# Two attention layers over a shared context: operand q placed by transfers, context normalised on GpSimd, a context load and the ternary weights moved

## The reference, cut to what matters

```
x: 8 x 56 x 128, ctx: 8 x 1500 x 128, 16 heads of 8
x = x + mha(ln(x), ln(x))                    # self-attention over 56 tokens
x = x + mha(ln(x), ln(ctx))                  # first pass: the context is normalised
x = x + mixture of 8 experts(ln(x))          # top 2
# second pass; the context goes in as it is, weights are ternary:
#   Wt = W + (clip(round(W / (mean|W| + eps)), -1, 1) * mean|W| - W)
x = x + mha(ln(x), ctx; weights Wt)
```

## Time and profile before

| | |
|---|---|
| time, median of 3 runs | 639.55 us (637.69 to 640.61) |
| the profiled execution | 638.79 us, of which its span is 637.0 us |
| busy, share of the span | PE 85%, DVE 67%, ACT 51%, POOL 24% |
| chain that ended last | PE 45%, DVE 23%, issue 21%, DMA 4%, POOL 3% |
| granted PE clock, mean | 0.935 |

### The profile page before, as it was taken

One profiled execution on the slowest core, in us unless ns is written; L12 is line 12 of the kernel. 1 busy time (PEld: TensorE's weight loads), 2 busy tenths in 40 slices (PEclk: granted clock), 3 DMA queues, 4 the chain that ended last, 5 costly groups with the idle time before them and its releaser, 6 DMA issues.

```text
span 637.0 us, 16158 instructions
## 1 busy us (share of the span) xinstructions
PE 544.5 (85%) x6582; PEld 383.9 (60%) x6582; DVE 425.6 (67%) x1090; ACT 326.7 (51%) x495; POOL 152.7 (24%) x128
## 2 busy tenths in 40 slices
PE   0699838589999999999967989468999999999996
PEld 0587515266766667676745767234666767667674
DVE  5667478679998999977224302569787687786730
ACT  0165214356666576765743333215566567676573
POOL 1554212313241524300015100223041240421000
PEclk9899668889999999999997989878999999999998
DMA  5010733434436353342200642026536436353300
GB/s 154 32 50 1 164 92 69 126 88 110 132 74 172 72 139 75 75 99 50 100 1 1 170 108 66 9 84 146 137 80 175 121 77 168 88 137 75 74 3 15
DMA packets 25338, 57.44 MB, mean 90 GB/s; under 512 B 4660, under 2 KB 8876, under 8 KB 25268
## 3 DMA queue, kind: packets, MB, share of 16 engines
q1 hardware_dynamic: 25268, 56.45, 34.6%
HBM read 17.81 MB, written 0.23 MB: 28 GB/s over the span
## 4 chain that ended last, share of the span: by engine, by line
PE 45%; DVE 23%; issue 21%; DMA 4%; POOL 3%; ACT 2%; SPq 2%; DVEq 0%; POOLq 0%; ACTq 0%
DVE mxp L791 11%; PE SM L1170 10%; PE PO L1185 9%; PE ST L1149 6%; PE MI L1101 6%; DMA cx<-in_ctx 3%; PE MI L1091 3%; DVE cx L779 3%; DVE qst L815 2%; PE MI L1125 2%; PE SM L1257 2%; DVE ksplit L786 1%; DVE cstat L763 1%; PE SM L1125 1%; DVE xn L732 1%
## 5 line engine op out<-in xcount | busy, mean ns | idle before, releaser
L791 DVE TENSOR_REDUCE mxp<-SM 112x1 f32<-112x500 f32 x364 | 235.2, 673 | 60.5 <-PE SM L1170 59.1
L593 ACT ACTIVATE PT<-ST 128x896 f32<-128x896 f32 x192 | 171.1, 911 | 49.7 <-PE ST L1149 49.1
L1170 PE MATMUL SM<-kst,qst 96*112 96x500 bf16 x364 | 143.1, 407 | 24.7 <-DVE mxp L791 24.1
L1149 PEld LDWEIGHTS ST<-qst,kst 98*128 98x128 bf16 x1536 | 95.0, 100 | 32.6 <-issue 9.7
L1149 PE MATMUL ST<-qst,kst 98*128 98x112 bf16 x1536 | 108.5, 215 | 1.2 <-DMA qst<-mrow 1.2
L471 POOL TENSOR_TENSOR kr<-kf,ksplit 128x500 f32<-128x500 f32 x48 | 56.1, 1170 | 184.4 <-ACT ksplit L565 184.3
L1185 PE MATMUL PO<-PT,vaug 125*32 125x112 f32 x3072 | 96.5, 264 | 2.1 <-ACT PT L593 1.5
L1170 PEld LDWEIGHTS SM<-kst,qst 96*112 96x112 bf16 x364 | 46.8, 131 | 66.9 <-DVE mxp L791 55.2
L1185 PEld LDWEIGHTS PO<-PT,vaug 125*32 125x32 f32 x3072 | 70.5, 110 | 24.5 <-issue 14.9
L577 ACT ACTIVATE vaug<-MI 125x512 f32<-125x512 f32 x48 | 28.7, 598 | 79.4 <-PE MI L1101 79.4
L476 POOL TENSOR_TENSOR ksplit<-kr,ksplit 128x500 bf16<-128x500 f32 x48 | 54.5, 1135 | 53.4 <-DVE ksplit L786 53.4
(11 more groups left out here) (129 smaller groups left out, 555.4 us busy)
## 6 DMA issues: line engine op xcount, KB each, us to landing
kst<-ksplit SPq DMA_DIRECT2D x192, 187.5 KB, 3.8
cx<-in_ctx SPq DMA_DIRECT2D x8, 750.0 KB
xT<-in_ctxT SPq DMA_DIRECT2D x8, 750.0 KB, 4.6
moe<-in_w1T SPq DMA_DIRECT2D x8, 256.0 KB, 2.9
moe<-in_w2T SPq DMA_DIRECT2D x8, 256.0 KB, 3.3
qall<-qsplit SPq DMA_DIRECT2D x12, 112.0 KB, 2.3
watt<-in_watt SPq DMA_DIRECT2D x1, 768.0 KB, 5.8
qst<-mrow SPq DMA_DIRECT2D x32, 1.8 KB
```

Source lines behind the costliest of these rows:

```text
L593: nc.scalar.activation(PT[:, k % PTB], ST[:, k % 2, :, 0:4 * PC], ACT.Exp, scale=SCALE).then_inc(exp_done, 1)
L791: nc.vector.tensor_reduce(mxp[:, j // 3, j % 3:j % 3 + 1], tile_bank(j, banks), AX.X, ALU.max).then_inc(sm_red, 1)
L1149: last = mm(ST[:, k % 2, cc, PC * p:PC * (p + 1)], kst[n.par][:, 4 * half + p, at:at + 128], qst[n.par][:, 4 * half + p], start=True, stop ...
L1170: mm(tile_bank(j, banks), qst[n.par][0:SROWS, j // 3], kst[n.par][0:SROWS, j // 3, at:at + THIRD], start=True, stop=True).then_inc(sm_full, 1)
```

## The change

1. **q by transfers.** For every unit but the first of a pass, SP copies `qall` into `qst` (`place`, two transfers for each half: 48 rows x 4 pairs x 56 bf16). POOL clears `qst` once at the start, so that the zeros are there. PE waits on `q_placed` in place of `qst_ready`.
2. **Normalising on POOL.** The twelve instructions for each of the units 3 to 7 move to POOL, behind `ctx_rstd`. DVE waits for them before it overwrites the statistics in the next window. Units 0 to 2, before the windows, stay on DVE.
3. **Context loads.** In the program a window now loads the context of n + 4, at its end, and unit 3 is loaded before the experts' weights, ahead of the first pass.
4. **Ternary weights** are made in W5, after the tiles of step 6.

```diff
+            def place(n, half):
+                if n.c == 1:
+                    sp.wait_ge(qall_loaded, 16 * TERMS * (n.s + 1))
+                if n.s or n.c >= 2:
+                    sp.wait_ge(st_full, (n + -2).count(STEPS, HSTEP * (half + 1)))
+                pairs = slice(4 * half, 4 * half + 4)
+                for hh in range(2):
+                    rows_of = slice(hh * DH * TERMS, (hh + 1) * DH * TERMS)
+                    sp.dma_start(qst[n.par][rows_of, pairs, L * hh:L * (hh + 1)],
+                                 qall[rows_of, pairs, L * n.c:L * (n.c + 1)]).then_inc(q_placed[half][n.par], 16)
...
             def window(n):
-                if n.s == 0 and (n + 3).exists():
-                    load_ctx(n + 3)
                 if (n + 1).exists():
+                    place(n + 1, 1)
                     restack(n + 1, 1)
                 shift(n, 1)
                 if (n + 2).exists():
+                    place(n + 2, 0)
                     restack(n + 2, 0)
                 if (n + 1).exists():
                     shift(n + 1, 0)
+                if n.s == 0 and (n + 4).exists():
+                    load_ctx(n + 4)
...
             restack(u0, 1)
+            load_ctx(Unit(0, None, 3))
             load_expert(0, 0)
...
             shift(u0, 0)
+            place(u1, 0)
             restack(u1, 0)
...
+                nc.gpsimd.memset(qst[s][0:SROWS], 0.0)
...
+            def ctx_normalise(n):
+                pool.wait_ge(crstd_ready, n.count(1, 1))
+                for i in range(3):
+                    for c in range(CPT * i, CPT * (i + 1)):
+                        last = nc.gpsimd.tensor_scalar(cx[n.par][:, c], cx[n.par][:, c], cmv[:, c, 0:1],
+                                                       crstd[:, c:c + 1], ALU.subtract, ALU.mult)
+                    last.then_inc(cn_ready, 1)
...
+                if ln_unit is not None:
+                    ctx_normalise(ln_unit)
...
                     if nxt.exists():
-                        if k == Q2_STEP:
-                            place_q(nxt, 1)
-                        if k == Q1_STEP and k_unit.exists():
-                            place_q(k_unit, 0)
...
+                    if n.s == 0 and n.c == B - 3 and k == HSTEP:
+                        ternary_weights()
...
                         if k == 5:
+                            if ln_unit.it is not None or ln_unit.c > 3:
+                                dve.wait_ge(cn_ready, (ln_unit + -1).count(3, 3))
                             ctx_aggregate(ln_unit)
-                        if k in (7, 8, 9):
-                            ctx_normalise(ln_unit, (k - 7,))
...
                     if j == 3:
                         place_q(first, 1)
-                    if j == START_TILES - 2:
-                        place_q(first + 1, 0)
```

More of the change, by code:

```diff
@@ L303, in build_kernel @@
             sem("mparts_ready"), sem("mx_full"), sem("mx_evac"))
+        q_placed = [[sem(f"q_placed{h}{p}") for p in range(2)] for h in range(2)]
         shift_loaded = [[sem(f"shift_loaded{h}{p}") for p in range(2)] for h in range(2)]
@@ L429, in _ @@
             shift(v0, 0)
+            place(v0 + 1, 0)
             restack(v0 + 1, 0)
@@ L810, in place_q @@
                     dve.wait_ge(ld_member, 32)
-                if n.s or n.it is not None or n.c >= 2:
+                if n.s:
                     dve.wait_ge(st_full, (n + -2).count(STEPS, HSTEP * (half + 1)))
@@ L836, in add_projection, with ternary_weights @@
                                         ).then_inc(x_added, 1)
+            def ternary_weights():
+                dve.wait_ge(gam_ready, 1)
+                nc.vector.tensor_scalar(thr[:, 0], gam[:], EPS, 0.5, ALU.add, ALU.mult)
+                nc.vector.tensor_scalar(thr[:, 1], gam[:], EPS, -0.5, ALU.add, ALU.mult).then_inc(thr_ready, 1)
+                dve.wait_ge(thr_ready, 1)
+                for w in range(4):
+                    nc.vector.tensor_scalar(wt[:, 0, w], watt[:, 2, w], thr[:, 0, w:w + 1], None, ALU.is_gt)
+                    last = nc.vector.tensor_scalar(wt[:, 1, w], watt[:, 2, w], thr[:, 1, w:w + 1], None, ALU.is_lt)
+                last.then_inc(tern1, 1)
+                dve.wait_ge(tern1, 1)
+                nc.vector.tensor_tensor(wt[:, 0], wt[:, 0], wt[:, 1], ALU.subtract).then_inc(tern2, 1)
+                dve.wait_ge(tern2, 1)
+                for w in range(4):
+                    last = nc.vector.scalar_tensor_tensor(out=wt[:, 1, w], in0=wt[:, 0, w], scalar=gam[:, w:w + 1],
+                                                          in1=watt[:, 2, w], op0=ALU.mult, op1=ALU.subtract)
+                last.then_inc(tern3, 1)
+                dve.wait_ge(tern3, 1)
+                nc.vector.tensor_tensor(watt[:, 2], watt[:, 2], wt[:, 1], ALU.add).then_inc(wq_ready, 1)
             def window(n):
@@ L932, in _ @@
             split_q(0)
-            dve.wait_ge(gam_ready, 1)
-            nc.vector.tensor_scalar(thr[:, 0], gam[:], EPS, 0.5, ALU.add, ALU.mult)
-            nc.vector.tensor_scalar(thr[:, 1], gam[:], EPS, -0.5, ALU.add, ALU.mult).then_inc(thr_ready, 1)
-            dve.wait_ge(thr_ready, 1)
-            for w in range(4):
-                nc.vector.tensor_scalar(wt[:, 0, w], watt[:, 2, w], thr[:, 0, w:w + 1], None, ALU.is_gt)
-                last = nc.vector.tensor_scalar(wt[:, 1, w], watt[:, 2, w], thr[:, 1, w:w + 1], None, ALU.is_lt)
-            last.then_inc(tern1, 1)
-            dve.wait_ge(tern1, 1)
-            nc.vector.tensor_tensor(wt[:, 0], wt[:, 0], wt[:, 1], ALU.subtract).then_inc(tern2, 1)
-            dve.wait_ge(tern2, 1)
-            for w in range(4):
-                last = nc.vector.scalar_tensor_tensor(out=wt[:, 1, w], in0=wt[:, 0, w], scalar=gam[:, w:w + 1],
-                                                      in1=watt[:, 2, w], op0=ALU.mult, op1=ALU.subtract)
-            last.then_inc(tern3, 1)
-            dve.wait_ge(tern3, 1)
-            nc.vector.tensor_tensor(watt[:, 2], watt[:, 2], wt[:, 1], ALU.add).then_inc(wq_ready, 1)
             def start_pass(s):
@@ L1158, in scores, with q_here @@
                     output_forth(n + -1)
+            def q_here(n, half):
+                if n.c == 0:
+                    pe.wait_ge(qst_ready, 2 * n.s + half + 1)
+                else:
+                    pe.wait_ge(q_placed[half][n.par], 32 * (n.s * (3 + n.par) + n.c // 2 + n.par))
             def max_tile(n, j, banks=2):
                 if j == 0:
-                    pe.wait_ge(qst_ready, n.count(2, 1))
+                    q_here(n, 0)
                     pe.wait_ge(kst_loaded[0][n.par], n.par_count(16 * TERMS, 16 * TERMS))
                 if j == TILES // 2:
-                    pe.wait_ge(qst_ready, n.count(2, 2))
+                    q_here(n, 1)
                     pe.wait_ge(kst_loaded[1][n.par], n.par_count(16 * TERMS, 16 * TERMS))
```

## The result

The changed kernel takes 654.79 us (median of 4 runs, 654.04 to 656.43), the kernel before, measured beside it, 640.08 (4 runs, 637.69 to 642.92). The ratio is 1.0231, interval 1.0183 to 1.028: slower clear of noise, though the interval doesn't settle whether by more than 2%. The forecast was 626.5, with a range of 619 to 635: wrong in sign and by 28 us.

The account below looks back on a forecast made before the run. PE and DVE both bound W0 to W4, PE sets the pace later; gains 9.3 + 4.6 + 0.9 - 5.3 + 0.3 + 3.2 = 13.0 us off the 639.55 median gave 626.5 us, range 619 to 635.

Parts of the forecast that it names:

- The step that failed: POOL's normalising instruction in the first pass: 0.4 us each, 4.8 for twelve, fitting the room before PE's transposes, costing nothing.
- GpSimd is the bound of the first pass: Rival: PE's last third waits 12t - 6.3 in five windows; 639 us at t = 0.73, 655 at 1.0; chance 0.10.
- the first (the clock stays up in W5): Rival: no clock fall behind W5's idle stretch, and DVE's relief is worth more; 622 us, chance 0.14.
- the third: Rival: operands `kst` and `qst` arrive late, each of 13 windows losing about half a us more; 633 us, chance 0.10.
- W0: First window of the first pass: early context load removes the wait, 40.30 to 31.0 us, a gain of 9.3.
- W1 to W4: First-pass windows: placing and normalising leave DVE, 27.86 to 26.7 us each, a gain of 4.6 in all.
- The start: Before the first scores: weights and a placing leave DVE, gain 0.9; wait for `qall` up to 1 us longer.
- The rival on the early load: The load in W0 pushes `qall` or something else back as much, so the wait stays; 636 us, chance 0.04.
- W5: First-pass window taking the ternary weights: PE idles 3.9 us, then a clock of 0.50; slower by 5.3 us.
- Second pass: Windows V0 to V6: V1 to V5 gain 0.57 each, V6 0.3, V0 nothing; gain 3.2 us in all.
- V0: First window of the second pass: no change, as placings go and the restack comes later; bounds -1 to +1 us.
- V5: Second-pass window, forecast with V1 to V4: 0.57 us less.

Follow-up runs that it names:

- Kernel 4: The changed kernel with POOL normalising only 128, 64 and 16 columns of each chunk in the three thirds: 640.59 us (one run).
- kernel 1: The changed kernel with the twelve normalising instructions of a window back on DVE: 635.42 us, ratio 0.9927.
- kernel 9: The kernel before with only the normalising of the windows moved to GpSimd: 665.66 us, ratio 1.0402.
- kernel 7: The kernel before with only the early load of unit 3's context, placed behind `qall`: 634.28 us, ratio 0.9926.
- kernel 11: The changed kernel with each third normalised on GpSimd by two instructions of 512 columns instead of four of 128: 634.47 us, ratio 0.991.
- kernel 3: The changed kernel with the load of unit 3's context moved behind `qall` in SP's queue: 653.31 us, ratio 1.0172.
- Kernel 10: The kernel before with only the ternary weights moved to W5: 645.25 us, ratio 1.0075.
- kernel 6: The kernel before with only the placing of q by SP's transfers, context loads where they were: 634.14 us, ratio 0.9911.
- 1 to 6: Includes two otherwise unlisted: the change with ternary weights at the start, 651.66 us; that plus normalising on DVE and unit 3's context behind `qall`, 629.66 us.
- 8: The changed kernel with wide normalising on GpSimd (two 512-column instructions a third), ternary weights at the start, unit 3's context behind `qall`: 628.77 us, ratio 0.9826.
- 12: The changed kernel with normalising on DVE, unit 3's context behind `qall` and the ternary weights in W7: 627.11 us, ratio 0.9794.

## Why the prediction was wrong

**The step that failed** is "with 0.1 for what is fixed, less than the whole fill, I take **0.4** ... At 0.4 it costs nothing". The instruction takes 0.796 us. Its own bounds, 0.20 and 1.13, held it, and the step also had the room right, 0.6 for each by the first third and 0.52 by the last. It then took a value just inside the room, from the slope of another operation and the fill's fixed cost, and costed the whole at nothing. Kernel 4 shows both halves of that wrong: 0.38 fixed, not 0.1, and 3.3 ns a column, not 2.3. The trace of before had a hint that I used only in a rival. The power takes 2.27 us for twelve columns, and the page of before has the same operation for four:

```profile
L459 POOL TENSOR_TENSOR xrstd<-xvar,half_neg 112x4 f32<-112x4 f32 x4 | 4.0, 1010 | 127.1 <-DVE xvar L729 127.1
```

A straight line through 1.01 at four and 2.27 at twelve leaves 0.38 at none. With a range of 0.20 to 1.13 that straddled the room of 0.52, the term did not deserve "nothing" but a price with a large chance.

**The rival that came true** is the second, "GpSimd is the bound of the first pass", with a chance of 0.10. Its formula, 12t - 6.3, gives 3.25 us a window at t = 0.796 (3.0 with the 9.33 that the twelve take together); the rows show 3.4. By the formula alone the time would be 626.5 + 5 x 3.25 = 643; kernel 1 shows that the part is worth 19.4 us and kernel 9 that it is worth 25.2 by itself. The difference is the clock, which the rival left out although and the earlier trace rows showed a low clock behind two idle stretches of PE. That the rival's time at t = 1.0, 655, is the one measured is luck: the instruction takes 0.8, and the 28 us of the miss are 18.3 in W1 to W4, 13.6 of them waits for POOL, 5.1 at the start, and the rest in the other stretches. "GPSIMD Engine Reference" of the Trainium skill, section 8, "Key points", with DVE about twice as fast, gave an estimate of 0.73 from DVE's 366 ns; the ratio measured is 796 / 366 = 2.2, so that rule agrees. The roughly line rate for one input of the same page of the Trainium skill, section 4.1, "Engine selection", does not hold for this instruction, with two scalars a row and 128 columns. I set the two statements against each other, and believed the one that suited the sum. Of the other rivals, the first (the clock stays up in W5) did not come true: W5 ran at 0.85. Nor did the third: for `qst` and `kst` together PE waits 1.2 us for transfers in the whole kernel, as before.

**W0**: 31.0 forecast, 33.1 measured, 30.65 with the early load alone (kernel 7). The load did remove the context wait. The trace has 2.1 us of waits for POOL's thirds at its end (0.39 and 1.66), and a clock of 0.93.

**W1 to W4**: 26.7 forecast for the moves on DVE. That was right for what it priced: 27.36 in kernel 11, where PE waits for POOL four times by up to 0.7, and less those 0.65 a window it is 26.7. With DVE normalising it is 26.98, so moving the normalising was worth 0.3 us a window at best, and the placing 0.9; I had 0.45 and 0.6 or a little more. The prize for the risky half of the change was about 1.2 us over the four windows.

**The start**: "up to 1 us longer" for the 750 KB ahead of `qall`. It was 4.6 (kernel 3). Nothing in the step bounded it; the page of before had a bound, in part 6 (size, median us from issue to landing), where another load of this size takes 4.6 us:

```profile
xT<-in_ctxT SPq DMA_DIRECT2D x8, 750.0 KB, 4.6
```

The rival on the early load, at 0.04, named this mechanism; its other half, that the wait in W0 stays, did not come true.

**W5**: +5.3 forecast, +6.8 measured; the idle stretch 4.12 against 3.9, the low clock as said, though it begins while PE still idles (0.57 from 292 to 294). Kernel 10, where nothing from POOL comes before, has +5.8 without the placing's gain, so the step was right to about 0.1; in the changed kernel W5 also begins at a low clock, left by W4's waits.

**Second pass**: 0.57 a window forecast, 0.61 measured in V1 to V4 (25.55 to 24.94). V0 became 0.3 longer, inside its bounds. V5 was forecast with the others at 0.57 less and is 0.3 longer: the next section. V7 and the end cost 2.0 more at a clock of 0.85 against 0.93, which was not foreseen. Kernels 7, 9 and 10, without any placing by SP, have V0 at 29.0 to 29.1 and V7 with the end at 27.1 to 27.5, so V0's 0.3 and most of the 2.0 are not shown to come from the change.

The parts, each measured alone, are -4.9 (kernel 6), -4.7 (kernel 7), +4.8 (kernel 10) and +25.2 (kernel 9), in sum +20.4 where the whole is +14.7. Kernel 7's load stands behind `qall`; with the change's own order, 4.6 us worse at the start, the sum would be further off. Most of the gap is in W1 to W4: GpSimd's normalising makes them 22.2 us longer in kernel 9 (against before) and 17.5 in the changed kernel (against kernel 1), with nearly the same waits for POOL but a lower clock in kernel 9 (0.90 to 0.96 against 0.91 to 1.00). Why the clock fell more often there is not shown.

## What to carry to other kernels

Before work goes to another engine, set its time against the slack at the point where it is read, and where the price of the instruction is only bounded, ask on which side of the slack most of the bounds lie; a single value just inside it is no price. On GpSimd here the number of instructions counts nearly as much as their columns, and the same normalising in wide pieces was worth 20 us. A wait of PE costs more than its length when the clock falls behind it, and a block on a helper engine belongs in a stretch where that engine has no tiles in front of PE (W7, not W5).

## What was not expected of the hardware

- **GpSimd's scalar instruction** has a fixed part of 0.38 us and 3.1 to 3.3 ns a column (794, 580 and 429 ns at 128, 64 and 16 columns), while its two-input instruction of 512 columns takes 1.04 us, 2.0 ns a column with everything. Two wide ones (2.08) beat four narrow ones (3.18), though they pass over the data twice. How much of that is the smaller number and how much the kind of instruction, no run shows.
- **The same wait does not always cost the same.** Three windows of equal work differ by 2.6 us in the changed kernel (30.34, 30.77, 32.95, at clocks of 1.00, 0.97 and 0.91), each with the same 3.4 us of waits. Whether the clock falls behind such a wait is not the same from window to window, and the runs don't show what decides it.
- **The placings make a load late in V5.** In the second pass the transposed context `xT` comes by transfer, and PE waits for it there once, for 0.3 to 1.5 us, in every kernel with placings by SP (after, and 1 to 6, 8, 11 and 12) and in none of those without (before, 7, 9 and 10). In the changed kernel the wait stands in PE's timeline as

```profile
578.47 1.08 PE L1120 MATMUL MI<-xT,watt 128*128 128x500 f32 x2 [0.68 <-DMA xT<-in_ctxT]
```

  The timeline of SP in kernel 6, which has only the placings, and PE's wait there, point to the reason: the load is issued behind a placing and a restack, 5.3 us before PE wants it and 3.2 before V5 begins, where the kernel before issues it 5.7 ahead of V5, at 556.68.

```profile
545.46 1.60 SPq L393 DMA_DIRECT2D qst<-qall  x2
547.18 5.00 SPq L379 DMA_DIRECT2D kst<-ksplit  x6
552.22 0.68 SPq L399 DMA_DIRECT2D qst<-mrow  x1
552.94 0.50 SPq L339 DMA_DIRECT2D xT<-in_ctxT  x1
```

```profile
559.04 1.08 PE L1115 MATMUL MI<-xT,watt 128*128 128x500 f32 x2 [0.84 <-DMA xT<-in_ctxT]
```

  The load's own start was not moved in an experiment.
